# A four-layer graph network on one core: destination windows of 8 nodes in place of 16, batches of 16 tiles, and new owners for the row traffic

## The reference: what is computed

```python
x = norm(x + L0(x))   # 3 steps: out = clip(0.9 * segment_sum(norm_e * out[src], dst) + 0.1 * x, 0, 1)
x = norm(x + L1(x))   # 6 steps: msg_e = out[src] @ W_e, summed by dst, then a GRU cell
                      #   W_e = (relu(edge_attr_e @ en1.T) @ en2.T).reshape(32, 32), another matrix for every edge
x = norm(x + L2(x))   # degree-normed graph convolution, one weight matrix
x = norm(x + L3(x))   # the same with self loops, no weight
```

## Time and profile before

| | |
|---|---|
| median of 3 runs | 33,394.66 us |
| the profiled execution | 33,337.04 us, its span 33,335.2 us |
| busy in the span | PE 20,515.9 us (62%), POOL 18,336.2 (55%), DVE 10,580.6 (32%), ACT 10,378.6 (31%) |
| mean granted TensorE clock | 0.794 of full |
| moved | 2,085 MB, 63 GB/s on average |

### The profile page before, as it was taken

How to read it: one execution, slowest core, us unless ns; L and a number is a source line. 1 busy time by engine, 2 the same in 40 slices (tenths; PEclk the granted TensorE clock), 3 DMA queues, 4 the chain that set the end, 5 groups by cost and what they waited for, 6 DMA issues and landing times. The chain is left out here.

```text
span 33335.2 us, 544551 instructions
## 1 busy us (share of the span) xinstructions
PE 20515.9 (62%) x139272; PEld 8830.7 (26%) x139272; DVE 10580.6 (32%) x16070; ACT 10378.6 (31%) x27656; POOL 18336.2 (55%) x18855
## 2 busy tenths in 40 slices
PE   5556311111111999899989989998998999211111
PEld 3333200101101333333333333333333333101101
DVE  7665200000000444344344434443443444000000
ACT  0003201001001555455445545554554555101001
POOL 5882476574673664366066426615651662574673
PEclk8778655555555999999999999999999999555555
DMA  2114322222222333233233323323332332122222
GB/s 65 23 23 145 90 41 39 40 41 37 41 41 37 84 84 77 62 84 84 61 78 84 79 60 84 84 64 75 84 81 58 85 84 70 37 41 37 41 41 36
DMA packets 5284518, 2084.98 MB, mean 63 GB/s; under 512 B 4443107, under 2 KB 5028299, under 8 KB 5280836
## 3 DMA queue, kind: packets, MB, share of 16 engines
q1 hardware_dynamic: 4251184, 1592.54, 19.6%
q0 software_dynamic: 603136, 315.16, 6.7%
q10 hardware_dynamic: 430032, 175.29, 1.9%
HBM read 1533.08 MB, written 536.12 MB: 62 GB/s over the span
## 5 line engine op out<-in xcount | busy, mean ns | idle before, releaser
L699 POOL DMA_INDIRECT sb_xg<-node_rows,sb_idx x17248 | 16309.7, 946 | 13020.8 <-DMA sb_idx<-sb_src_c 7619.4
L823 PE MATMUL banks<-sb_spread,sb_eh_sb 128*128 128x512 f32 x23808 | 11823.6, 619 | 107.8 <-DMA sb_eh_sb<-eh 89.7
L778 DVE TENSOR_TENSOR sb_spread<-sb_xs,banks_p 128x2048 f32<-128x2048 f32 x2976 | 6720.0, 2286 | 9408.6 <-DMA sb_xs<-gathered_rows 6785.2
L888 ACT ACTIVATE sb_g<-banks 128x512 f32<-128x512 f32 x11904 | 6967.6, 597 | 5794.4 <-PE banks L823 5751.4
L803 PE MATMUL banks_s<-sb_mask,sb_xs 128*32 128x16 f32 x43648 | 991.4, 202 | 9194.7 <-DMA sb_xs<-gathered_rows 9194.7
L882 ACT ACTIVATE sb_s<-banks_s 32x32 f32<-32x32 f32 x10912 | 2055.7, 188 | 10677.5 <-PE banks_s L803 10257.5
L823 PEld LDWEIGHTS banks<-sb_spread,sb_eh_sb 128*128 128x128 f32 x23808 | 4044.7, 189 | 4884.2 <-issue 4154.9
L760 DVE TENSOR_TENSOR sb_mask<-sb_meta_t,sb_node 128x128 f32<-128x128 f32 x2728 | 787.9, 289 | 10504.1 <-PE banks_s L803 10370.0
L811 PE MATMUL banks_p<-sb_g,sb_en 128*32 128x256 f32 x47616 | 3796.8, 391 | 3.9 <-ACT sb_pj L897 3.9
L803 PEld LDWEIGHTS banks_s<-sb_mask,sb_xs 128*32 128x32 f32 x43648 | 719.5, 128 | 9432.5 <-issue 8608.6
L293 POOL DMA_INDIRECT slots<-sb_rows,sb_slot_u x1600 | 2024.3, 1265 | 725.2 <-issue 715.1
(11 more groups left out here) (201 smaller groups left out, 8888.0 us busy)
## 6 DMA issues: line engine op xcount, KB each, us to landing
sb_eh_sb<-eh SPq DMA_DIRECT2D x1488, 512.0 KB
sb_xs<-gathered_rows SPq DMA_DIRECT2D x21824, 16.0 KB, 1.7
sb_xg<-node_rows,sb_idx POOLq DMA_INDIRECT x17248, 2.4
gathered_rows<-sb_xg SPq DMA_DIRECT2D x2156, 128.0 KB, 1.7
eh<-sb_eh_sb ACTq DMA_DIRECT2D x248, 512.0 KB
parts<-sb_part ACTq DMA_DIRECT2D x2728, 16.0 KB, 1.6
sb_g<-parts SPq DMA_DIRECT2D x44, 992.0 KB
slots<-sb_zeros SPq DMA_DIRECT2D x16, 2294.0 KB, 45.8
```

The costliest lines, as they stand in the source:

```text
L699: nc.gpsimd.indirect_dma_start(m.xg[h][:, t * D:(t + 1) * D], None, m.node_dram, bass.IndirectOffsetOnAxis(ap=m.idx[h][:, t:t + 1], axis=0 ...
L778: V.tensor_tensor(m.spread[q], m.xs[h].rearrange("s (t i) -> s t i", i=D)[:, tiles, :].unsqueeze(3) .broadcast_to([P, TS, D, WN]), m.mask_ ...
L823: mm(m.ps_g[:, t % 4, :], m.eh[h][:, t * K:(t + 1) * K], m.spread[t // TS][:, t % TS, :, :], start=True, stop=True).then_inc(g_done, 1)
L888: nc.scalar.activation(m.g[h // 2][:, :, (h % 2) * TC + t, :], m.ps_g[:, t % 4, :].rearrange("k (i n) -> k i n", n=WN), copy).then_inc(g_s ...
```

## The change

The diff changes sizes, three stages and the owners of two duties.

- A window holds 8 nodes (784 windows, of which 782 have nodes), a batch 16 tiles; there are TP = 2432 tiles in 38 bodies, 152 batches. `spread` is still 2048 elements wide, but for 8 tiles; an outer product has 256 columns, and two tiles share a PSUM bank, which ACT copies in one go. `group` runs once per batch with 16 weight slices of 256 columns in place of 4 times with 4. `sum_rows` takes four tiles in one matmul (128 weight columns, 32 columns). `encode_edges` keeps batches of 8 and has 76 bodies.
- The place of an edge comes from two digits of its window: TensorE picks the running start of the window from a 49 x 16 table per column, and DVE counts how many earlier edges of the same column have the same window (16 instructions of 125 columns per half, both inputs in SBUF, plus one over 2000 columns). The 400-wide one-hots and their 48 matmuls per half are gone.
- `edge_pass` becomes `conv_pass` and `plain_pass`. In `conv_pass` POOL copies the index list itself, gathers groups of 16 rows, and stores the group before to `xg_dram` from its own queue after its 8th gather. In `plain_pass` ACT loads index lists and keeps the gathered rows, DVE makes ACT's former copies, and SP stores results. In both, SP fetches a tile batch when a count of landed groups, computed from the row number read from the table, has been reached; gathering and fetching are no longer tied group to batch. The hidden values come 1 MB at a time into two buffers.
- `owner` is no longer kept: `own_tiles` makes the window comparison on DVE, 19 chunks of 128 tiles per `add_tiles`, 8 matmuls of 256 columns each.

```diff
-WN = 16
+WN = 8
-HI, LO = 25, 16
+HI, LO = 49, 16
-TC, L, BODIES = 8, 4, 62
+TC, L, BODIES = 16, 4, 38
+JC, JBODIES = 8, 49
+EC, EBODIES = 8, 76
-OQ, OC = 124, 16
+OQ, OC = 128, 19
...
 def scatter_rows(nc, m, attr):
+            def compare(i, half, h):
+                c = bass.ds(half * ST, ST)
+                V.tensor_copy(m.win_now[h], m.win[:, c]).then_inc(win_ready, 1)
+                onehots(nc, m.hot_shi[h], m.shi[:, c], m.iota, ST, NQ).then_inc(hots, 1)
+                onehots(nc, m.hot_slo[h], m.slo[:, c], m.iota, ST, NM).then_inc(hots, 1)
+                onehots(nc, m.now_hi[h], m.whi[:, c], m.iota, ST, HI).then_inc(hots, 1)
+                onehots(nc, m.now_lo[h], m.wlo[:, c], m.iota, ST, LO).then_inc(hots, 1)
+                V.tensor_scalar(m.hot_t[h], m.whi_row[h], m.pcol[0:HI, 0:1], None, ALU.is_equal).then_inc(hots, 1)
+                for t in range(ST):
+                    e = slice(t * EQ, (t + 1) * EQ)
+                    V.scalar_tensor_tensor(m.same[h][:, e], m.win_row[h][:, e], m.win_now[h][:, t:t + 1],
+                                           m.before[0:EQ, 0:EQ], ALU.is_equal, ALU.mult,
+                                           accum_out=m.ahead[h][:, t:t + 1]).then_inc(compared, 1)
...
+def conv_pass(nc, m, after):
+        @block.gpsimd
+        def _(pool):
+            def keep(i, b, h):
+                pool.wait_ge(got[h], i * GJ + GJ)
+                pool.dma_start(m.xg_dram[:, bass.ds(b * 2 * JC * D, 2 * JC * D)], m.xg_two[h]).then_inc(put[h], 16)
...
+                    nc.gpsimd.tensor_copy(m.idx_two[h], m.src_c[:, bass.ds(b * 2 * JC, 2 * JC)]).then_inc(listed, 1)
+                    for t in range(2 * JC):
+                        nc.gpsimd.indirect_dma_start(
+                            m.xg_two[h][:, t * D:(t + 1) * D], None, m.node_dram,
+                            bass.IndirectOffsetOnAxis(ap=m.idx_two[h][:, t:t + 1], axis=0)).then_inc(got[h], 16)
+                        if t == JC - 1:
+                            if h == 1:
+                                keep(i, b - 1, 0)
...
+        @block.sync
+        def _(sp):
+            def fetch(i, n, h):
+                for q in range(2):
+                    rows = rows_of_batch(nc, m, i, h, q)
+                    if q == 0:
+                        sp.wait_ge(summed, n + 1)
+                        sp.wait_ge(made, 2 * n + 2)
+                    sp.wait_ge(landed, ((rows[TS - 1] >> 4) & 127) + 1)
+                    for t in range(TS):
+                        sp.dma_start(m.xs[h][:, (q * TS + t) * D:(q * TS + t + 1) * D],
+                                     m.xg_dram[:, bass.ds(rows[t] * D, D)]).then_inc(loaded[h], 16)
+            def fetch_eh(i, n, h):
+                sp.wait_ge(g_done, (n - 1 + L) * U)
+                sp.dma_start(m.eh[h % 2], m.eh_dram[:, bass.ds(n * TC * K, TC * K)]).then_inc(eh_in[h % 2], 16)
...
+            def outer(i, n, h):
+                for u in range(U):
+                    for v in range(2):
+                        t = 2 * u + v
+                        o = mm(m.ps_pair[u % 4][:, v, :, :], m.eh[h % 2][:, t * K:(t + 1) * K],
+                               m.spread[t // TS][:, t % TS, :, :], start=True, stop=True)
+                    if u == U // 2 - 1:
+                        first = (h % 2) * D // 2
+                        last = group(range(first, first + D // 2), 1 - h // 2)
```

More of the change, by code:

```diff
@@ L850, in fold @@
                 mm(m.ps_out, m.s[h], after, start=False, stop=True).then_inc(folded, 1)
[L852 to L864 removed]
+            skewed(pe, (fold, 4), (sum_rows, 0), (outer, 0), tail=last_group)
         @block.scalar
@@ L918, in add_tiles @@
 def add_tiles(nc, m):
-    with phase(nc, "parts_a", "parts_b", "parts_c", "parts_d", "agg") as (block, *sems):
-        parts_in, agg, per = sems[0:4], sems[4], OC // 4
+    with phase(nc, "parts_a", "parts_b", "parts_c", "parts_d", "named", "agg") as (block, *sems):
+        parts_in, named, agg = sems[0:4], sems[4], sems[5]
+        bounds = (0, 5, 10, 15, OC)
         @block.sync
@@ L1087, in turn @@
 def turn(nc, m, pe, x, out_i, turned, turned_sb):
-    for c in range(NC):
-        s = out_i * NC + c
+    for c in range(NB):
+        s = out_i * NB + c
         if s >= 2:
@@ L1247, in _ @@
             do = Chain(dve, own)
-            for c in range(NC):
-                part = slice(c * WN * D, (c + 1) * WN * D)
+            for c in range(NB):
+                part = slice(c * PW * D, (c + 1) * PW * D)
                 do(V.tensor_tensor(m.h[:, part], m.agg[c], m.y[:, part], ALU.add))
@@ L1352, in build @@
-            place_windows(nc, m)
-            scatter_rows(nc, m, attr)
+            with ExitStack() as stage:
+                sb = make(stage)
+                m.src, m.dst, m.tmp_i = (sb(n, [EQ, ET], I32) for n in ("src", "dst", "tmp_i"))
+                m.wcol = sb("wcol", [EQ, ET])
+                m.iota_i, m.pcol_i = sb("iota_i", [P, NW], I32), sb("pcol_i", [P, 1], I32)
+                prepare_edges(nc, m, src, dst, weight)
+            with ExitStack() as stage:
+                sb = make(stage)
+                m.cnt, m.tiles, m.scan0, m.scan1, m.first, m.first_slot = (
+                    sb(n, [P, NW]) for n in ("cnt", "tiles", "scan0", "scan1", "first", "first_slot"))
+                m.cnt_i = sb("cnt_i", [P, NW], I32)
+                m.tnum, m.begun, m.row_of_i = sb("tnum", [P, 1]), sb("begun", [OQ, 1]), sb("row_of_i", [OQ, OC], I32)
+                m.hot_hi = sb("hot_hi", [EQ, HT, HI], BF16, halves=2)
+                m.hot_lo = sb("hot_lo", [EQ, HT, LO], BF16, halves=2)
+                m.rows_t = sb("rows_t", [RT, 8, 4 * EQ], F16)
+                count_windows(nc, m)
+                place_windows(nc, m)
@@ L1394, in build @@
         m.pj = sb("pj", [P, 2 * P], halves=2)
[L1395 removed]
+        spread = spread.rearrange("p h t i n -> p (h t i n)")
+        m.own_p = [spread[0:OQ, h * NW:(h + 1) * NW] for h in range(2)]
+        spare = spread[:, 0:32 * NQ].rearrange("p (a g q) -> p a g q", a=2, q=NQ)
         m.turned_m, m.turned_h = spare[:, 0], spare[:, 1]
```

761 lines of the change are left out of this document (428 added, 333 removed).

## The result

The changed kernel takes 29,621.46 us, the median of 4 runs (29,617.48 to 29,626.81), against 33,393.89 before: a ratio of 0.887, 95% interval 0.8855 to 0.8886. The forecast was 30,220 us, its range 29,450 to 31,900. The profiled execution took 29,624.24 us, its span 29,622.5, which is 3712.7 less than the span before.

A forecast was written before the change was run, and what follows sets the result against it. Conv passes were bound by TensorE, plain passes and scatter by GpSimd, the plain tail by SP. 33,337 + 530 (setup) - 2838 (conv) - 870 (plain) = 30,159 us profiled, median 30,220; range 29,450 to 31,900.

The forecast's parts named there:

- the forecast's own: Range of the main case for the whole kernel, 29,700 to 30,800 us, given chance 0.58.
- Weight loads hidden: Conv-pass outer products: weight loads hide behind 256-column matmuls of 0.21 us; rival of unhidden loads, 31,280 us, chance 0.06.
- TensorE's 11.6 us a batch: Conv passes: outer products with group chunks 9.92, folds 0.56 and new sums 1.12 us per batch of 16 tiles.
- the slower rival: Conv passes: TensorE's clock stays at the 1.2 GHz level, +6400 us, 36,620 us in all; chance 0.03.
- GpSimd's store, 1.55 us: Conv passes: POOL's 256 KB store per group, within 22.3 us a group; rival of 4.5 us, 32,210 us, chance 0.13.
- SyncE's 11 us, "below both": Conv passes: SP's fetches, table reads and 1 MB load take 11 us a batch, below POOL's and PE's times.
- The last test that I named: Conv passes: forecast wrong if batches wait for SP, not POOL, before nine tenths of a pass.
- Plain passes: Five plain loops fall from 2261 to 2075 us as SP fetches while POOL gathers; -870 us with `add_tiles`.
- The +12 us for `add_tiles`: Node work of each pass: 304 instructions of 0.21 us for 128 of 0.43, and DVE's window comparison, +12 us.
- Setup: Stages before the passes: larger one-hots, window comparisons, encoding, packing and scatter contention (+270) add +530 us together.
- DMAs of over 2.5 us: Scatter: sign that DVE's one-hots shut POOL out, POOL DMAs this long expected once per half.
- +860 us: Scatter: POOL shut out for all 11.7 us, +8.6 a half; rival total 30,810 us, chance 0.12.

The follow-up runs named there:

- E5: Changed kernel with twelve semaphore increments put once into SyncE's code ahead of conv_pass, outside every loop; 29,201.96 us, ratio 0.8747.
- E6: Kernel before, with only the changed kernel's plain_pass owners, in batches of 8; tiles of 16 nodes and conv_pass kept; 32,072.30 us, ratio 0.9608.
- E9: E5 with the sixteen scatter comparisons of each half run twice, the first time into spare tiles; 29,354.83 us.
- E12: Changed kernel with four semaphore increments once ahead of conv_pass, in place of E5's twelve; 47,600.68 us on a slower chip.
- E4: Changed kernel with one more semaphore increment ahead of each store of SyncE's plain loop, its body four instructions longer; 46,645 us on a slower chip.
- E3: Changed kernel with the edge matrices' load of a batch right behind that batch's fetch, one batch earlier; 47,537 us on a slower chip.
- E2: Changed kernel without the four semaphore increments ahead of the edge matrices' loads in SyncE's conv loop body; 46,690 us on a slower chip.

## Why the prediction was right, and where it was not

Predicted 30,220, measured 29,621: inside the range, just past the low end of the forecast's own. The mechanism held for the first two thirds of a conv pass, in which GpSimd takes over from TensorE. In the last third it was SyncE's queue that did, and that the total lay inside the range all the same was partly luck.

**Weight loads hidden: right.** With data at hand 16 of the new matmuls take 3.70 us, 0.23 each (0.21 forecast). PE's rows of E5 in three late batches:

```profile
12647.67 6.52 PE L870 MATMUL banks<-sb_spread,sb_eh_sb 128*128 128x256 f32 x16 [1.25 <-DMA sb_eh_sb<-eh]
...
12655.99 3.72 PE L870 MATMUL banks<-sb_spread,sb_eh_sb 128*128 128x256 f32 x16
...
12660.80 3.70 PE L870 MATMUL banks<-sb_spread,sb_eh_sb 128*128 128x256 f32 x16
...
12671.05 0.40 PE L897 MATMUL banks_s<-sb_fold,sb_pj 128*128 128x32 f32 x2 [1.04 <-ACT sb_pj L933]
...
12672.41 3.70 PE L870 MATMUL banks<-sb_spread,sb_eh_sb 128*128 128x256 f32 x16
...
12682.72 3.70 PE L870 MATMUL banks<-sb_spread,sb_eh_sb 128*128 128x256 f32 x16
...
12694.33 5.38 PE L870 MATMUL banks<-sb_spread,sb_eh_sb 128*128 128x256 f32 x16
```

**TensorE's 11.6 us a batch: met, but not by its terms.** A batch with nothing slow in it takes 12682.72 - 12672.41 = 10.31 us, 1.3 less than the sum. Most often every second one is 11.61 (12694.33 - 12682.72), with a wait of 1.04 us for ScalarE's copy, which the sum didn't have, and one in which the clock falls takes up to 12.0. The average of 11.5 to 11.7 is made of these.

**The clock: the slower rival did not come, its seed did.** The clock stays at 0.83 in the gathers and 0.91 after them, nowhere near 1.2 GHz throughout. But the 6.52 above follow a wait, and the 3.70 none. In the changed kernel the batch at 15121.92 has 6.65 us behind a wait of 2.71. That agrees with the Trainium skill ("TensorE: Matmul & The Clock Gate", "HAM oscillation — how this bites in real kernels"), which has TensorE fall back to the slow clock when it waits for data. It is not the whole of it: the 5.38 at 12694.33 have only a wait of 1.04 us for ScalarE a little before them, and the 3.70 at 12672.41 have the same. The slow clock lengthens late batches by up to 2.9 us; that it costs nothing while GpSimd sets the pace, as I wrote, no run shows by itself.

**GpSimd's store, 1.55 us: the term that was mis-sized.** It measures 0.59 on average over 588. I had taken a gather for the nearest row, but a plain DMA costs GpSimd an issue and little more. The group is 21.3 us, not 22.3, and the gathers 2091, not 2185: -94 a pass. SyncE's plain issue of 0.33 to 0.36 was the nearer row.

**SyncE's 11 us, "below both": the step that failed.** The sum was right: 11.0 to 11.5 us is what a batch takes SyncE in E5 when nothing holds it up, and 10.9 to 11.4 in three batches out of four in the changed kernel. It left out the stall, which brings the average to 12.8, above TensorE's 11.6. SyncE then decides from about two thirds of the pass on, not nowhere, and each conv loop is 67 us longer than E5's. The last test that I named, SP being what batches wait for before nine tenths of a pass, has come out against me, and two errors hid each other: loop 2323 forecast, 2305 measured, made of -94 and +67 among others. Without the stall the loop would have been 2238, and the total 29,202, below my range. The low end was too high.

**Plain passes: right.** Tail of 100 us, loop 2060 for 2075. E6 adds what I hadn't worked out: the smaller tiles work against this part. The +12 us for `add_tiles` did not come: from the end of a conv loop to the next store of node rows it is 136 us before and after.

**Setup: +338 for +530.** The start of the scatter is 50 us later (68 forecast), what follows it took 208 more (192). The scatter took 81 more, not 270, and all of that is GpSimd's busy time, 2106.16 - 2024.33 = 82. The rows show why. Beside the comparisons and beside the one-hots:

```profile
1500.56 0.33 DVE L374 SCALAR_TENSOR_TENSOR sb_same<-sb_win_row,sb_win_now,sb_before 125x125 bf16<-125x125 f16 x1
1500.65 1.31 POOL L343 DMA_INDIRECT slots<-sb_rows,sb_slot_u  x1 [0.30 <-issue]
...
1502.27 1.18 POOL L343 DMA_INDIRECT slots<-sb_rows,sb_slot_u  x1 [0.31 <-issue]
...
1507.22 1.79 DVE L168 TENSOR_TENSOR sb_hot_shi<-sb_shi,sb_iota 125x1568 bf16<-125x1568 f32 x1
1508.24 1.83 POOL L343 DMA_INDIRECT slots<-sb_rows,sb_slot_u  x1 [0.30 <-issue]
1508.93 1.22 DVE L168 TENSOR_TENSOR sb_hot_slo<-sb_slo,sb_iota 125x1024 bf16<-125x1024 f32 x1
1510.07 0.97 DVE L168 TENSOR_TENSOR sb_now_hi<-sb_whi,sb_iota 125x784 bf16<-125x784 f32 x1
1510.38 1.72 POOL L343 DMA_INDIRECT slots<-sb_rows,sb_slot_u  x1 [0.30 <-issue]
```

Sixteen comparisons of 0.34 us, 0.27 apart, let most of GpSimd's DMAs through at 1.18 to 1.31 us; by the trace they cost 0.7 us a half, and E9 says 0.5 for another sixteen. The longer one-hot block costs 1.4 a half, little more than the shorter (1.2): GpSimd's DMA gets in between its instructions, 1.83 and 1.72 us, where I had it shut out to the block's end as in the earlier trace rows. DMAs of over 2.5 us, the sign that I had named, did not come; the longest takes 2.35. The rule of the Trainium skill ("SBUF — State Buffer", "Who interferes with whom"), by which a VectorE instruction with two SBUF inputs contends with GpSimd's reads, and the second to start is shut out for the whole instruction (this last part the Trainium skill says of VectorE's two-port modes), agrees for one instruction and must not be carried over a row of them: taken so, it gave +860 us, and 81 came.

## What to carry to other kernels

When work is spread over more, smaller tiles, count each queue's issues anew, and read the period of its loop over whole turns, the backward branch included: here the spare queue became the bound. When a queue's loop is late by the same amount at each turn, look at the page's instruction queues, and move the body by a dozen instructions before redesigning anything. Change one owner or one size at a time if you want to know what each gives: the owners were worth 1310 us in the plain passes, and the tiles cost 300 of them.

## What the runs showed of the hardware

**A loop body is fetched anew at each turn, or not, by its place.** The same 271 recorded instructions stall 5.2 us and about 1.0 us per turn in the changed kernel and in E12, and not in E4 and E5, where they stand 12 instructions further on. Length may enter as well: E3's 272, which start 2 later than in the changed kernel, stall, and E2's 267, which start 7 earlier, do not. With the stall, that instruction queue moved (9.49 - 0.88) MB / 216 turns = 40 KB a turn. Whether 5 to 11 instructions would do, and what border the body crosses, was not tried.

**On two of four chips SyncE crawls while GpSimd gathers.** There the change is a loss: 46,645 to 46,690 us without the stall and 47,537 to 47,601 with it, for 43,041 and 43,089 before (ratios 1.084 and 1.105). SyncE's queue in a plain pass of E4, during the gathers and after them:

```profile
5850.82 71.85 SPq L1014 DMA_DIRECT2D sb_xs<-gathered_rows  x16
...
7001.15 9.18 SPq L1014 DMA_DIRECT2D sb_xs<-gathered_rows  x16
```

GpSimd at the same time:

```profile
5846.26 1.09 POOL L982 DMA_INDIRECT sb_xg<-node_rows,sb_idx  x1 [0.30 <-issue]
5847.66 1.09 POOL L982 DMA_INDIRECT sb_xg<-node_rows,sb_idx  x1 [0.30 <-issue]
```

A gather comes mostly every 1.40 us, not every 1.25, and most of SyncE's records, address arithmetic too, start at multiples of 0.70 us from one another, half of that; 16 fetches take 72 us for 9. Only 24 of a plain pass's 152 batches are summed when the gathers end, where it is 143 in the changed kernel's own profile. Kernels that issue more per pass from SyncE (2432 fetches for 1984) lose more there, which fits the ratios; but of the kernel before there is no trace from such a chip, and what couples the two engines was not found.
